# Expert stage of an eight-stage kernel: two blocks at a time instead of one, and two PSUM banks for the down sum

## What is computed

```python
x = x + tanh(g_ffn[2]) * _L2_ffn_ref(_layernorm(x), ...)

def _L2_ffn_ref(hidden_states, gate_w, gate_bias, expert_gate, expert_up, expert_down, shared_gate, shared_up, shared_down):
    # 32 experts, top 8, 4 groups of experts of which the best 2 count
    topk_idx, topk_w = _gate(x, gate_w, gate_bias)   # sigmoid(x @ gate_w.T), group choice, top 8, normalise, * 2.5
    g = jnp.einsum('th,eih->eti', x, expert_gate)
    u = jnp.einsum('th,eih->eti', x, expert_up)
    outs = jnp.einsum('eti,ehi->eth', jax.nn.silu(g) * u, expert_down)
    final = (gathered * topk_w[:, :, None]).sum(1)
    return final.reshape(orig_shape) + shared          # shared: the same silu(g) * u form, unweighted
```

## Time and profile before

| | |
|---|---|
| median of 3 runs | 3493.46 us (3490.92 to 3500.74) |
| profiled execution, device time | 3487.68 us |
| its span | 3485.9 us |
| busy over the span | PE 92%, PEld 65%, DVE 67%, ACT 43%, POOL 34% |
| expert stage, first to last down product | 1861.4 to 2526 us |
| the 547 us of its inner part (1902 to 2449) | PE busy 536.6, DVE 424.8, ACT 182.5 us, granted clock 1.00 |

### The profile page before, as it was taken

The page is one execution under the profiler, slowest core; times in us unless marked ns, Lnnn a source line. Parts: engine busy times, 40 slices in busy tenths (PEclk is TensorE's granted clock), DMA queues, the critical chain, the costliest instruction groups (busy, mean ns, idle before and its releaser), DMA issues. The chain is left out here.

```text
span 3485.9 us, 73820 instructions
## 1 busy us (share of the span) xinstructions
PE 3194.5 (92%) x26410; PEld 2250.5 (65%) x26410; DVE 2319.7 (67%) x6096; ACT 1511.4 (43%) x2832; POOL 1169.9 (34%) x1359
## 2 busy tenths in 40 slices
PE   5999879999999999669998999999999999999978
PEld 3666535455556666447676888888866666666646
DVE  3666655666645555558877777777677877787733
ACT  2655511111115556236663333333255555555533
POOL 3555310000005555334430000000056665666532
PEclk9999989999999999769998999999999999999989
DMA  4000056566560000011102333333200000000001
GB/s 148 8 9 9 3 162 183 151 191 178 161 162 9 8 9 7 1 47 25 25 18 92 102 101 98 98 99 104 92 16 7 9 7 9 7 9 7 5 16 33
DMA packets 109400, 211.52 MB, mean 61 GB/s; under 512 B 18608, under 2 KB 28976, under 8 KB 108752
## 3 DMA queue, kind: packets, MB, share of 16 engines
q1 hardware_dynamic: 104848, 200.26, 19.4%
q10 hardware_dynamic: 4416, 9.59, 0.9%
HBM read 198.24 MB, written 5.77 MB: 59 GB/s over the span
## 5 line engine op out<-in xcount | busy, mean ns | idle before, releaser
L355 PE MATMUL ps<-parts 96*128 96x512 f32 (+1 forms) x1568 | 668.7, 426 | 12.9 <-DVE work L1663 7.4
L357 PE MATMUL ps<-parts 96*128 96x512 f32 (+1 forms) x1568 | 618.1, 394 | 0.0
L356 PE MATMUL ps<-parts 96*128 96x512 f32 (+1 forms) x1568 | 616.3, 393 | 0.0
L325 POOL TENSOR_TENSOR rstd<-mv,eps 128x4 f32<-128x4 f32 x144 | 30.0, 208 | 1374.8 <-DVE mv L308 1374.7
L740 ACT ACTIVATE work<-ps 128x512 f32<-128x512 f32 x512 | 305.8, 597 | 394.2 <-PE ps L357 367.5
L355 PEld LDWEIGHTS ps<-parts 96*128 96x128 f32 (+1 forms) x1568 | 296.5, 189 | 107.7 <-issue 43.7
L1616 ACT ACTIVATE work<-ps 128x512 f32<-128x512 f32 x272 | 162.5, 597 | 454.0 <-PE ps L357 453.8
L703 PEld LDWEIGHTS ps<-work 64*64 64x64 f32 x8192 | 221.6, 133 | 207.8 <-issue 207.8
L357 PEld LDWEIGHTS ps<-parts 96*128 96x128 f32 (+1 forms) x1568 | 295.8, 189 | 67.0
L849 DVE TENSOR_REDUCE work<-work 128x8 f32<-128x512 f32 (+1 forms) x256 | 175.6, 686 | 232.4 <-ACT work L752 232.0
L356 PEld LDWEIGHTS ps<-parts 96*128 96x128 f32 (+1 forms) x1568 | 297.6, 190 | 44.8
(11 more groups left out here) (282 smaller groups left out, 5700.3 us busy)
## 6 DMA issues: line engine op xcount, KB each, us to landing
work<-gate_rows SPq DMA_DIRECT2D x128, 512.0 KB, 5.6
work<-expert_rows SPq DMA_DIRECT2D x512, 128.0 KB, 2.9
work<-gate_rows SPq DMA_DIRECT2D x128, 256.0 KB, 7.6
work<-in_ctxT SPq DMA_DIRECT2D x72, 192.0 KB, 2.3
out<-x SPq DMA_DIRECT2D x16, 256.0 KB, 2.3
work<-work SPq DMA_DIRECT2D x224, 16.0 KB
work<-work SPq DMA_DIRECT2D x16, 128.0 KB, 3.2
early<-in_l0f_w ACTq DMA_DIRECT2D x1, 1536.0 KB, 13.9
```

Source lines behind the costliest of these rows:

```text
L355: T.matmul(out, lh, rh, start=True, stop=False)
L356: T.matmul(out, lh, rl, start=False, stop=False)
L357: return T.matmul(out, ll, rh, start=False, stop=True)
```

## The change

The TensorE takes two blocks at a time: gate and up of two blocks, then down of two. `aT` gets a third slot (`AR = 3`). The down sum gets two banks, one for even and one for odd groups, and the addition to x moves from the end of a group's body to step j = 2 of the next one; the last group's stands behind the loop. Router and exponential move from j = 1 to j = 2, the VectorE's routing parts from 2 <= j < 9 to 3 <= j < 10, the norm's two parts from 9 and 11 to 10 and 12. The loop is now `by_twos` over pairs of groups: the first pair written out, a loop, the last pair written out. As a pair of groups has 34 blocks, the TensorE's pairs of blocks fall on even j in an even group (A) and on odd j in an odd group (B); in an even group a pair spans its last block and the next group's first.

```diff
+def by_two_groups(eng, n, body):
+    def both(it, last):
+        for u in range(2):
+            body(it * 2 + u, u, last)
+    by_twos(eng, n // 2, both)
...
-    WR = 8
+    WR, AR = 8, 3
...
-    sg, aT = [w([GT]), w([GT])], [w([GT]), w([GT])]
+    sg, aT = [w([GT]), w([GT])], [w([GT]) for _ in range(AR)]
...
-    acc, ps_x = c.ps[:, 6, :], c.ps[:, 7, :]
+    acc, ps_x = (c.ps[:, 4, :], c.ps[:, 5, :]), c.ps[:, 7, :]
...
+    def downs_before(g, j):
+        last = j - AR if j >= AR else {0: NB - 2, 1: NB - 1, 2: NB - 3}[j] - NB
+        return g * NB + last + 1
...
             def down(g, u, j):
-                m, b = at(g, u, j)
+                m = g * NB + j
                 te.wait_ge(a_ready, m + 1)
                 if j == 0:
-                    te.wait_ge(added, g + 1)
+                    need(te, added, g - 1)
...
                 for j in range(NB):
-                    if not (end and j + 2 >= NB):
-                        gate_up(*ahead(g, u, j))
+                    pair = (u * NB + j) % 2 == 0
+                    for k in (2, 3):
+                        if pair and not (end and j + k >= NB):
+                            gate_up(*ahead(g, u, j, k))
                     if j == 0 and not end:
                         transposes(g + 1)
-                    if j == 1 and not end:
+                    if j == 2 and not end:
                         router(g + 1, 1 - u)
                     if j == 11 and not end:
                         turn_weights(g + 1, 1 - u)
-                    down(g, u, j)
+                    if pair:
+                        down(g, u, j)
+                        down(*ahead(g, u, j, 1))
...
-                    if j == 1 and not end:
+                    if j == 2 and not end:
                         sigmoid_exp(g + 1)
...
             def mult(g, u, j):
                 m, b = at(g, u, j)
                 ve.wait_ge(silu_ready, m + 1)
-                if not (isinstance(g, int) and g == 0 and j < 2):
-                    if j < 2:
-                        ve.wait_ge(y_ready, g) if j == 1 else ve.wait_ge(down_done, g * (NB - 1))
-                    else:
-                        ve.wait_ge(down_done, g * (NB - 1) + (j - 1))
-                out = V.tensor_tensor(aT[b], sg[b], ps_u[b], ALU.mult)
+                if not (isinstance(g, int) and g == 0 and j < AR):
+                    ve.wait_ge(down_done, downs_before(g, j))
+                out = V.tensor_tensor(aT[j % AR], sg[b], ps_u[b], ALU.mult)
...
-                    if 2 <= j < 9 and not end:
-                        for part in range(2 * j - 4, min(2 * j - 2, 13)):
+                    if 3 <= j < 10 and not end:
+                        for part in range(2 * j - 6, min(2 * j - 4, 13)):
                             routing(g + 1, 1 - u, part)
-                    if j == 9 and not last_pair:
+                    if j == 10 and not last_pair:
                         norm.take_moments(ve, g + 2)
-                    if j == 11 and not last_pair:
+                    if j == 12 and not last_pair:
                         norm.scale(ve, g + 2)
-                ve.wait_ge(y_ready, g + 1)
+                    if j == 2 and not (isinstance(g, int) and g == 0):
+                        add(g - 1, 1 - u)
+
+            def add(g, u):
+                ve.wait_ge(down_done, g * NB + NB)
...
```

More of the change, by code:

```diff
@@ L1495, in experts @@
     ps_g, ps_u = (tuple(c.ps[:, i + j, :] for j in range(2)) for i in (0, 2))
-    acc, ps_x = c.ps[:, 6, :], c.ps[:, 7, :]
+    acc, ps_x = (c.ps[:, 4, :], c.ps[:, 5, :]), c.ps[:, 7, :]
     norm = Norm(c, "f2_ln", hn)
     sem = lambda s: c.sem("f2_" + s)
-    x_ready, x_out, gu_ready, silu_ready, u_read, a_ready, y_ready, added, link = (
-        sem(s) for s in ("x", "x_out", "gu", "silu", "u_read", "a", "y", "added", "link"))
+    x_ready, x_out, gu_ready, silu_ready, u_read, a_ready, added, link = (
+        sem(s) for s in ("x", "x_out", "gu", "silu", "u_read", "a", "added", "link"))
     down_done, wts_ready, norm_link = sem("down"), sem("wts"), sem("norm_link")
@@ L1534, in body @@
                     spread(g + 1, 1 - u)
-            by_pairs(sp, n, body)
+            by_two_groups(sp, n, body)
         @block.gpsimd
@@ L1576, in down @@
             def down(g, u, j):
-                m, b = at(g, u, j)
+                m = g * NB + j
                 te.wait_ge(a_ready, m + 1)
                 if j == 0:
-                    te.wait_ge(added, g + 1)
+                    need(te, added, g - 1)
                 for t in range(TG):
-                    last = T.matmul(acc[:, t * D:(t + 1) * D], aT[b][:, t * P:(t + 1) * P], c.w["l2f_d"][:, j, :],
+                    last = T.matmul(acc[u][:, t * D:(t + 1) * D], aT[j % AR][:, t * P:(t + 1) * P], c.w["l2f_d"][:, j, :],
                                     start=(j == 0 and t == 0), stop=(j == NB - 1), skip_group_check=True)
-                last.then_inc(y_ready if j == NB - 1 else down_done, 1)
+                last.then_inc(down_done, 1)
             te.wait_ge(c.l2f_in, 48)
@@ L1602, in body @@
                         turn_weights(g + 1, 1 - u)
-                    down(g, u, j)
-            by_pairs(te, n, body)
+                    if pair:
+                        down(g, u, j)
+                        down(*ahead(g, u, j, 1))
+            by_two_groups(te, n, body)
         @block.scalar
@@ L1626, in take_weights @@
                 A.activation(wT[u][0:NE2, :], ps_x[0:NE2, :], ACT.Copy).then_inc(x_out, 1)
-            act.sem_inc(added, 1)
             act.wait_ge(c.l2f_in, 48)
@@ L1644, in body @@
                         take_weights(g + 1, 1 - u)
-            by_pairs(act, n, body)
+            by_two_groups(act, n, body)
         @block.vector
@@ L1672, in weight @@
                 ve.wait_ge(wb_in[j % WR], (g * (NR // WR) + (j // WR + 1)) * 32)
-                V.tensor_tensor(aT[b], aT[b], wb[j % WR], ALU.mult).then_inc(a_ready, 1)
+                V.tensor_tensor(aT[j % AR], aT[j % AR], wb[j % WR], ALU.mult).then_inc(a_ready, 1)
             def block_of(g, u, j):
@@ L1770, in body @@
                         split(g + 1, 1 - u)
-                    if 2 <= j < 9 and not end:
-                        for part in range(2 * j - 4, min(2 * j - 2, 13)):
+                    if 3 <= j < 10 and not end:
+                        for part in range(2 * j - 6, min(2 * j - 4, 13)):
                             routing(g + 1, 1 - u, part)
-                    if j == 9 and not last_pair:
+                    if j == 10 and not last_pair:
                         norm.take_moments(ve, g + 2)
-                    if j == 11 and not last_pair:
+                    if j == 12 and not last_pair:
                         norm.scale(ve, g + 2)
-                ve.wait_ge(y_ready, g + 1)
+                    if j == 2 and not (isinstance(g, int) and g == 0):
+                        add(g - 1, 1 - u)
+            def add(g, u):
+                ve.wait_ge(down_done, g * NB + NB)
                 xg = norm.xg(g)
-                V.scalar_tensor_tensor(out=xg, in0=acc.rearrange("p (t c) -> p t c", c=D), scalar=c.w["tg"][:, 6:7], in1=xg,
+                V.scalar_tensor_tensor(out=xg, in0=acc[u].rearrange("p (t c) -> p t c", c=D), scalar=c.w["tg"][:, 6:7], in1=xg,
                                        op0=ALU.mult, op1=ALU.add).then_inc(added, 1)
-            by_pairs(ve, n, body)
+            by_two_groups(ve, n, body)
+            add(n - 1, 1)
 def by_twos_and_two(eng, n, body):
```

## The result

The median of 5 runs is 3511.63 us (3502.88 to 3512.21), against 3493.46 before. The ratio is 1.0042, with a 95% interval of 1.0029 to 1.0054: 10 to 19 us slower. I had forecast 3497 and no measurable change. The median lies 2.6 above my range of 3483 to 3509. By the ratio, which makes it 3508.1 (3493.46 x 1.0042), it lies just inside. The slower side had only 0.16 of my chances.

The account below looks back on a forecast made before the run. The TensorE's pace was taken to bound the stage. New stalls of 29.3 us less 26.0 won (old stalls 12.0 and 11.3, seams 2.7) gave +3.3, so a median of 3497 us, range 3483 to 3509.

Parts of the forecast that it names:

- What bounds it: Expert stage's inner part: it goes at the TensorE's pace, busy 536.6 of 547 us, with the VectorE at 78%.
- the 26 I put on them and the seams: Whole stage: about 26 us could be won, 11.3 in add waits, 12.0 beside the routing, little in seams.
- Seams: TensorE's switches between kinds of product: a pair takes 4.51 against 4.53, 0.02 per seam saved, 2.7 us in all.
- Two banks: First down product of a group no longer waits for the addition to x: 11.3 us go, 0.75 a group.
- the cover I named: Moved addition on the VectorE costs nothing, since the VectorE waits there for block 5's silu; uncovered, about 10 us at most.
- Even groups, 2.0 us: TensorE waits for mult in even groups: 0.1 at block 7, 1.3 at block 9, 0.6 at block 11.
- odd groups, 1.5: TensorE waits in odd groups: 0.1 at block 8, 0.8 at block 10, 0.6 at block 12.
- The walk: Step-by-step timing of blocks beside the routing in the new order; its three stalls each within 0.3 to 0.4.
- The jump back, "up to 0.3 late": Odd-to-even passage: VectorE's loop return makes mult 2 up to 0.3 late; with mult 0's 0.13, 0.4 a passage.
- "The first pair, written out ... nothing": Stage's first pair of groups, written out instead of looped, runs the same instructions and costs nothing.
- A sign that failed: VectorE idle time behind down products would be mostly gone if the forecast was right.
- The clock rival: Stage's inner part: idle waits lower the TensorE's granted clock, 12 falls of 1.5 us, 18 us, 3515; chance 0.12.

Follow-up runs that it names:

- run 5: Changed kernel with one block at a time, no loop, VectorE routing parts dealt out by length, router, turned weights and norm parts moved: stage 660.3 us, ratio 0.9924.
- run 3: Kernel before with only two banks for the down sum, the addition at j = 2 and the loop this needs: stage 682.0 us, ratio 0.9999.
- run 1: Changed kernel with all eight pairs of groups written out, no loop: stage 687.2 us, ratio to before 1.0008.
- run 4: Changed kernel with router and exponential at j = 1 instead of 2 in even groups: stage 688.0 us, ratio 1.0013.
- 9: Changed kernel, pairs and loop kept, with routing dealt out by length and router, turned weights and norm parts moved: stage 664.2 us, ratio 0.9942.
- run 7: Changed kernel with the first two blocks of the first group in the old order: stage 693.8 us, ratio 1.0038.

## Why the prediction was right or wrong

The direction of the small loss was right, and the range just held by the ratio, but the sum was too small: the stage was to lose 3.3 us and lost 13.0. Three terms were missing or far too small (the jump back, the looped code, the first pair), and the range had been made for errors of other ones.

- **What bounds it** was right: in one step after another the TensorE waits for mult of two blocks before, and nothing else. With these waits removed (run 5) the stage lost 23.6 us, near the 26 I put on them and the seams.
- **Seams**: 4.52 a pair for 4.51. Right, and little: two single blocks take 4.53 (run 5), so a pair saves 0.01 and not 0.02, under 2 us instead of 2.7.
- **Two banks**: the 0.67 us a group went (0.75 with the restart behind it). In the changed kernel's trace idle time of the VectorE follows the addition, the cover I named, and run 3 shows its price in the old order.
- **Even groups, 2.0 us**: 2.14 in group 14, where no jump back precedes (0.13 of it the walked wait at the passage); odd groups, 1.5: 1.5, but only 1.3 in written-out code (run 1). The walk held to 0.2 in both, with block 9 a little under it (1.17 for 1.32) and block 11 too (0.34 for 0.57, 0.13 of restart behind each). Its reason held also (run 4, group 14): the exponential behind the second block starts the backlog.
- **The jump back, "up to 0.3 late"**: this is the step that failed. It measured 0.7 to 1.3 before block 4 of groups 4 to 12, 5.2 us in all, where the sum had about 0.3 in each of seven passages. I took its length from the 2.38 of the earlier trace rows and let it begin where the VectorE went idle. It measures 2.9 to 3.5. And I had it hidden "under the add wait": what covered it before was the router too, which the change moved behind block 5 in even groups. With the router before block 4 the wait is nearly gone, add wait or not (runs 3, 4 and 9).
- **Looped code**: some 4.5 us more stand in the loop without a jump, at block 11 of even groups and spread over odd ones. The walk has no such term, and its cause stays open; run 1 took it away together with the jump's.
- **"The first pair, written out ... nothing"**: 2.8 us, the second failed step. I looked at the loop's steady state and not at the stage's first blocks, where the new order puts a whole block at half the clock ahead of the first down (run 7 gave 2.7 back). Some 0.7 of it is weight 0's transfer, which landed later.
- **A sign that failed**: the VectorE's idle time behind down products is not "mostly gone". It is 64.4 us in the inner part, against 90.9 before.
- **The clock rival** didn't come: waits of 1.0 us, one or two a group, left the granted clock at 1.00 in the inner part. The stage was 96% busy. The Trainium skill (TensorE: Matmul & The Clock Gate, A second HAM failure mode) tells of a kernel in which short idle spells between groups of matmuls make the clock swing. The trace of this stage's inner part shows no such swing.
- The sum: +3.3 forecast for the stage, +13.0 measured. With 9.7 by the loop and 2.8 at the start it would be 15.8. Of the 2.8 too much about 1.9 are the jump's share of the 0.4 a passage, which I had counted already; the rest is spread over the walked terms. Without the loop (run 1) the stage stands 3.3 over the kernel before, the sum's own figure. That is luck: the start, which the sum had at nothing, is made up for by passages without a jump and by shorter stalls in odd groups.

## What to carry to other kernels

Before putting the TensorE's work in longer runs, price a seam between the kinds of product. Here it is 0.01 us a pair, so the longer runs could win hardly anything, while the second block of each run asks its supplier to be a down product (0.8 us) earlier. An engine that is 78% busy and still makes the bottleneck wait may have its work in lumps, as here: deal it out by length against the spare time per step (0.94 us here) before changing buffers or order. When work moves, ask what it had covered: the router helped to hide the VectorE's jump back, and no row of the kernel before shows that as a wait.

## What the runs showed of the hardware that I had not expected

- At the jump back of a loop of this size the VectorE stands idle for 2.7 to 3.5 us in the runs with the loop (3.49 above), and for 2.2 to 2.9 in the kernel before, where the addition stood before it. The trace puts it down to other engines or to "issue". In the runs with three slots, where no jump stands before mult 2, it is idle there for 0.6 us or less. Whether its length depends on the code's size or on the transfers beside it wasn't tried.
- Eight router records and the plain products behind them cost 0.08 to 0.09 us more than their own pitch in every kernel; transposes do not.
- A table load on the ScalarE runs ahead of the wait of the activation behind it. It did so in the changed kernel as well: the load ended at 2132.66, the exponential waited 0.36 for the router, and the next silu came 1.59 behind the exponential's start (1.59 in the earlier trace rows as well). The drain that the Trainium skill (ScalarE: Activation LUTs, What ACT_TABLE_LOAD costs) adds to a switch is not there in either trace:

```profile
2131.38 1.28 ACT L1639 ACT_TABLE_LOAD   x1
2133.03 0.28 ACT L1639 ACTIVATE work<-ps 128x128 f32<-128x128 f32 x1 [0.36 <-PE ps L1569]
2133.32 1.28 ACT L1634 ACT_TABLE_LOAD   x1
2134.62 0.60 ACT L1634 ACTIVATE work<-ps 128x512 f32<-128x512 f32 x1
```
